# A two-layer adaLN block on one core: the order of VectorE's small root steps in the first attention

## The chip, the core and the metric

The kernel runs on one core of a Trainium2 chip. The metric is the device time of one execution in microseconds. Before the change, three runs gave 1322.71, 1323.15 and 1325.7 us; the median is 1323.15.

Engines are called as in the profile: PE is TensorE, DVE is VectorE, ACT is ScalarE, POOL is GpSimd, SP is the queue that issues the DMAs.

## The reference, cut to what matters

Two layers, each an attention and a feed-forward part, over x of shape 32 x 256 x 128. Only the first attention matters here. For each of the 32 sequences:

```python
h = _layernorm(x, axis=-1) * (1 + ca) + sa
# inside _L0_attn_ref, whose x is h
x_norm = _layernorm(x, gamma, beta)
q = (x_norm @ w_q).reshape(B, T, HEADS, HEAD_DIM).transpose(0, 2, 1, 3)
k = (x_norm @ w_k).reshape(B, T, HEADS, HEAD_DIM).transpose(0, 2, 1, 3)
v = (x @ w_v).reshape(B, T, HEADS, HEAD_DIM).transpose(0, 2, 1, 3)
q = _l2_normalize(q)
k = _l2_normalize(k)
align = jnp.einsum('bhqd,bhkd->bhqk', q, k)
resonance = 0.5 + 0.5 * jnp.tanh((align - COLLAPSE_THRESHOLD) * SHARPNESS)
```

There are thus two norms in front (of x, then of the modulated h) and a division of every query and key by its length. The gates of q and k, the product with v, the output projection and the gated residual follow.

## The kernel before, in words

The first attention works on one sequence b of 256 rows (two tiles of 128) per turn. It is a software pipeline written out by hand: in turn b, ACT computes the tanh of the scores of sequence b, PE the scores and heads of b, while the sequences b + 1, b + 2 and b + 3 are prepared and b - 1 and b - 2 are finished. Each engine has its own `step(b, p)`, called by `stepped` (line 76 ff.) for b = -3 to 33: the turns up to 3 and from 28 are unrolled, the 24 turns from 4 to 27 run as a hardware loop of two turns per round. Every engine's instructions run in the order in which its `step` issues them, and semaphores hold them until what they need is there. The change touches DVE's `step` alone.

What DVE does in a turn, in its order (names as in the profile; the lines are those of the helpers):

- `stats_1`, `norm_1a` (L429, L440): statistics and moments of x for b + 3. POOL then computes 1/sqrt(variance + eps) in `rstd` (L403 add, L407 power), which gives `a_rstd`.
- `residual`, `heads_out`, `values`, `logits_out` (L854, L848, L829, L810): outputs of PE for b - 2, b - 1, b + 1 and b + 2. `logits_out` is a copy of 128x64.
- `norm_1b` (L446): the normalised tiles `a_xhat` of x for b + 3, two instructions. They wait for `a_rstd`. POOL waits for them and runs a row of four larger instructions: `a_scaled` (L414), `a_h` (L419), `a_wo_gated` (L706) and the sum into X (L708).
- `square_sums` (L748): sums over 8 of the squares of q and k of b + 2, 64 per row. The squares come from ACT (L656).
- nine `newton_step`s: the reciprocal root of these 64 sums. Step 1 clamps (L754, `a_norm2c`), step 2 makes an integer seed (L758, `a_seed`), steps 3 to 9 are small products on 128x64 tiles (L761, L763, L765, L768, L771, L773, L777). Each waits for the semaphore of the one before.
- `keys_out`, `queries_out` (L836, L841): copies of the turned keys and queries `a_kT` and `a_qT` of b + 1 from PSUM.
- `stats_2`, `norm_2a` (L429, L438, L440): statistics and moments of h for b + 3. POOL answers again with L403 and L407.
- `norm_2b` (L446): the tiles `a_xn`. PE waits for them and for `a_h` in `turn` (L523), which stands ahead of the scores of the next turn in its queue.
- `scale`, `gate_sums`, `turned_out`, `split_high`, `split_low`, `double_keys`: the normalised q and k, and their two f16 parts.

The steps with `norm` and `stats` exist while b + 3 is a sequence, so up to b = 28. POOL's `gate_out` (L706, L708) runs from b = 0. POOL's order in a turn is `norm_1`, `modulate`, `gate_out`, `norm_2`, `double_queries`. SP loads `a_mod_norm` for a later sequence once `a_h` is done.

Of the kernel before, what the change touches and what calls it, by code (L numbers as in the profile page):

```python
# [60 lines left out]
def wait(eng, sem, n):  # L61

    if isinstance(n, int) and n <= 0:
        return
    eng.wait_ge(sem, n)  # L65
# [228 lines left out]
def attention_0(nc, ctx, dram, sbuf, psum):  # L294
# [72 lines left out]
    def tile(b, t):  # L367
        return X[:, bass.ds(b * TT + t, 1), :] if not isinstance(b, int) else X[:, b * TT + t:b * TT + t + 1, :]
# [10 lines left out]
    def there(b):  # L379
        return not isinstance(b, int) or 0 <= b < B  # L380
# [62 lines left out]
    def standardise(dve, n, src, dst, mom, rstd, rstd_done, done):  # L443
        dve.wait_ge(rstd_done, n + 1)
        for t in range(TT):
            last = nc.vector.tensor_scalar(dst[:, t, :], src(t), mom[:, t, 0:1], rstd[:, t:t + 1], ALU.subtract, ALU.mult)  # L446
        last.then_inc(done, 1)

    def stats_1(dve, n):
        if isinstance(n, int) and n < FIRST:  # L450
            dve.wait_ge(dram["first_x_loaded"][n], 16)
        else:
            dve.wait_ge(x_loaded, (n - FIRST) * 16 + 16)
        wait(dve, moments1_done, n)
        for t in range(TT):
            statistics(n, lambda t: tile(n, t)[:, 0, :], stats1, stats1_done, t)

    def norm_1a(dve, n):
        moments_of(dve, n, stats1, moments1, stats1_done, moments1_done, xhat_done)

    def norm_1b(dve, n):

        wait(dve, scaled_done, n)
        standardise(dve, n, lambda t: tile(n, t)[:, 0, :], xhat, moments1, rstd1, rstd1_done, xhat_done)

    def stats_2(dve, n, t):
        if t == 0:
            dve.wait_ge(h_done, n + 1)
            wait(dve, moments2_done, n)
        statistics(n, lambda t: h[:, t, :], stats2, stats2_done, t)  # L470

    def norm_2a(dve, n):
        moments_of(dve, n, stats2, moments2, stats2_done, moments2_done, xn_done)

    def norm_2b(dve, n):

        wait(dve, turned, n)
        standardise(dve, n, lambda t: h[:, t, :], xn, moments2, rstd2, rstd2_done, xn_done)
# [9 lines left out]
    def run():  # L488
        with nc.Block() as block:
# [247 lines left out]
            def _(dve):  # L737
                def turned_out(n, p):
                    dve.wait_ge(turned, n + 1)

                    wait(dve, vl_psum, n)
                    nc.vector.tensor_copy(hT[p][:, :], PT[:, 0:T]).then_inc(hT_done, 1)
                    nc.vector.tensor_scalar(xnT[:, :], PT[:, T:2 * T], gammacol[:, :], betacol[:, :], ALU.mult, ALU.add).then_inc(xnT_done, 1)

                def square_sums(n):
                    dve.wait_ge(squares_done, n + 1)
                    wait(dve, newton, n * RSQRT_STEPS)
                    nc.vector.tensor_reduce(norm2[:, :], squares[:, :, :], AX.X, ALU.add).then_inc(norm2_done, 1)  # L748
# [32 lines left out]
                def scale(n):  # L781
                    dve.wait_ge(newton, n * RSQRT_STEPS + RSQRT_STEPS)
                    wait(dve, lo_done, n)
                    nc.vector.tensor_tensor(qkn[:, :, :, :].rearrange("p k t (h d) -> p t k h d", d=HD),
                                            PQ.rearrange("p (t k h d) -> p t k h d", t=TT, k=2, d=HD),
                                            rnorm[:, :].rearrange("p (t k h) -> p t k h", t=TT, k=2).unsqueeze(4).broadcast_to([P, TT, 2, H, HD]),
                                            ALU.mult).then_inc(qkn_done, 1)
# [19 lines left out]
                def logits_out(n):  # L807
                    dve.wait_ge(vl_psum, n + 1)
                    wait(dve, gate_in_done, n)
                    nc.vector.tensor_copy(logits[:, :], PL).then_inc(logits_done, 1)  # L810
# [13 lines left out]
                def values(n, p):  # L824
                    dve.wait_ge(vl_psum, n + 2)
                    dve.wait_ge(gates_done, n + 1)

                    wait(dve, heads_done, n * G - G)
                    nc.vector.tensor_tensor(vdiag[p], PV.rearrange("p (a r d) -> p a r d", r=G, d=HD),  # L829
                                            gate_k[:, :].rearrange("p (a r) -> p a r", r=G).unsqueeze(3).broadcast_to([P, TT * G, G, HD]),  # L830
                                            ALU.mult).then_inc(values_done, 1)

                def keys_out(n, p):
                    dve.wait_ge(kstack_psum, n + 1)
                    wait(dve, scores_ready, n * CHUNKS - CHUNKS)
                    nc.vector.tensor_copy(kT[p][:, :, :].rearrange("p g k -> p (g k)"), PT16).then_inc(kT_done, 1)  # L836

                def queries_out(n, p):
                    dve.wait_ge(qstack_psum, n + 1)
                    wait(dve, scores_ready, n * CHUNKS - CHUNKS)  # L840
                    nc.vector.tensor_copy(qT[p][:, :, :].rearrange("p g k -> p (g k)"), PT16).then_inc(qT_done, 1)  # L841

                def heads_out(n):

                    dve.wait_ge(heads_done, n * G + G)
                    dve.wait_ge(gT_done, n + 1)
                    wait(dve, projected, n)
                    nc.vector.scalar_tensor_tensor(out=oT[:, :], in0=PO[:, 0:T], scalar=PO[:, T:UNIT], in1=gT[:, :],  # L848
                                                   op0=ALU.add, op1=ALU.mult).then_inc(oT_done, 1)

                def residual(n):
                    dve.wait_ge(projected, n + 1)
                    dve.wait_ge(x_biased, n + 1)
                    nc.vector.tensor_tensor(tiles(n), tiles(n), PP.rearrange("p (t d) -> p t d", t=TT), ALU.add).then_inc(x_done, 1)  # L854

                def step(b, p):
                    older, old, new, next_, turns = there(b - 2), there(b - 1), there(b + 1), there(b + 2), there(b + 3)
                    ahead = turns and not (isinstance(b, int) and b == -3)

                    def newton_of(*ks):  # L860
                        if next_:
                            for k in ks:
                                newton_step(b + 2, k)

                    if ahead:
                        stats_1(dve, b + 3)
                    if older:
                        residual(b - 2)
                    if ahead:
                        norm_1a(dve, b + 3)  # L870
                    if old:
                        heads_out(b - 1)
                    if new:
                        values(b + 1, 1 - p)
                    if next_:
                        logits_out(b + 2)
                    if ahead:
                        norm_1b(dve, b + 3)
                    if next_:
                        square_sums(b + 2)  # L880
                    newton_of(1)
                    if new:
                        keys_out(b + 1, 1 - p)
                    newton_of(2)
                    if ahead:
                        stats_2(dve, b + 3, 0)
                    newton_of(3)
                    if ahead:
                        stats_2(dve, b + 3, 1)
                    newton_of(4)  # L890
                    if ahead:
                        norm_2a(dve, b + 3)
                    newton_of(5, 6)
                    if new:
                        queries_out(b + 1, 1 - p)
                    newton_of(7, 8, 9)
                    if ahead:
                        norm_2b(dve, b + 3)
                    if next_:
                        scale(b + 2)  # L900
                        gate_sums(b + 2)
                    if turns:
                        turned_out(b + 3, 1 - p)
                    if next_:
                        split_high(b + 2, p)
                        split_low(b + 2, p)
                        double_keys(b + 2, p)
                    if isinstance(b, int) and b == B - 1:
                        bound_squares(dve)
# [2313 lines left out]
```

## Time and profile before

| what | value |
|---|---|
| median of three runs | 1323.15 us |
| the profiled execution | 1322.84 us, span 1321.0 us |
| PE busy | 1219.2 us (92%) |
| DVE busy | 1055.2 us (80%) |
| ACT busy | 933.7 us (71%) |
| POOL busy | 574.6 us (43%) |
| turns of the first attention (first to last tanh of scores) | 42.5 to 398.2 us |

The span is that of the engines' instructions; the time of an execution lies a little above it. The shares of busy time are means over all stages. The first attention takes a good quarter of the span, and in the middle of it, from 200 to 300 us, PE is busy for 94.92 us, DVE for 93.04, ACT for 89.37 and POOL for 49.32, at a granted clock of 1.00 of TensorE. Four queues are close to full there, so the timelines and the waits tell more than the shares. In a timeline a row is one instruction or a few equal ones in a row (xN): start, duration, engine, line, operation, output and inputs. A DVE instruction that waits for nothing is recorded as starting up to 0.1 us before the end of the one in front of it.

### The profile page before, as it was taken

How to read it: one execution, taken by the hardware profiler on the slowest of the kernel's cores; microseconds unless marked ns; L12 is line 12 of the kernel's file. 1: busy time of each engine (PE TensorE's matmuls, PEld its weight loads, DVE VectorE, ACT ScalarE, POOL GpSimd, SP SyncE). 2: the span in 40 equal slices, each digit the busy share in tenths (PEclk: the TensorE clock that was granted, in tenths of full speed). 3: DMA queues.
4: the chain of work that ended last, by engine and by line, in shares of the span. 5: the costliest groups of instructions: out<-in, count | busy, mean ns of one | idle time of the engine just before them, and what ended most of it. 6: DMA issues, size and time to landing. Idle time of an engine off the chain costs nothing. (4 is left out here: it accounts for less than half of the span.)

```text
span 1321.0 us, 39879 instructions
## 1 busy us (share of the span) xinstructions
PE 1219.2 (92%) x13717; PEld 810.3 (61%) x13717; DVE 1055.2 (80%) x2935; ACT 933.7 (71%) x1338; POOL 574.6 (43%) x793
## 2 busy tenths in 40 slices
PE   3899999999996899997899999999879999999998
PEld 1555555555543677776555555555458878778776
DVE  5899999999965787766899999999746777777763
ACT  0698888888892556552588878788747676766765
POOL 2455444445421243322343343343236565655653
PEclk7799999999997999999899999999979999999999
DMA  4311111111002222200200000000000000000000
GB/s 126 141 35 32 33 35 36 36 36 36 28 10 49 58 50 59 59 17 4 105 14 16 12 12 16 12 12 17 6 2 9 9 16 8 16 8 16 16 8 25
DMA packets 47965, 40.68 MB, mean 31 GB/s; under 512 B 5376, under 2 KB 46688, under 8 KB 47360
## 3 DMA queue, kind: packets, MB, share of 16 engines
q1 hardware_dynamic: 47872, 39.45, 10.7%
q8 instruction: 57, 0.93, 0.3%
q14 instruction: 36, 0.29, 0.1%
HBM read 35.09 MB, written 4.34 MB: 30 GB/s over the span
## 5 line engine op out<-in xcount | busy, mean ns | idle before, releaser
L2416 ACT ACTIVATE a_probs<-psum_all 128x1024 f32<-128x1024 f32 x256 | 248.4, 1024 | 69.5 <-PE psum_all L2315 69.4
L683 ACT ACTIVATE probs<-psum_all,biases 128x1024 f32<-128x1024 f32 x256 | 272.5, 1115 | 32.8 <-PE psum_all L589 32.0
L2798 PE MATMUL psum_all<-ffn_hi,weights_r 128*128 128x512 f32 x704 | 283.8, 403 | 9.7 <-issue 4.5
L2798 PE MATMUL psum_all<-ffn_lo,weights_r 128*128 128x512 f32 x704 | 277.4, 394 | 0.0
L2758 POOL TENSOR_TENSOR ffn_lo<-ffn_full,ffn_hi 128x512 fp32r<-128x512 f32 x143 | 186.9, 1315 | 134.3 <-ACT ffn_hi L2875 97.8
L2798 PEld LDWEIGHTS psum_all<-ffn_hi,weights_r 128*128 128x128 f32 x704 | 133.7, 190 | 51.2 <-DVE ffn_full L2959 9.6
L2798 PEld LDWEIGHTS psum_all<-ffn_lo,weights_r 128*128 128x128 f32 x704 | 133.9, 190 | 25.8
L602 PE MATMUL psum_all<-probs,vpad 128*32 128x257 f32 x2048 | 138.0, 387 | 0.3 <-ACT probs L683 0.3
L2329 PE MATMUL psum_all<-a_probs,vpad 128*32 128x256 f32 x2048 | 137.7, 387 | 0.2 <-DVE a_sums L2494 0.2
L2887 ACT ACTIVATE ffn_full<-psum_all,scales 128x512 f32<-128x512 f32 x128 | 88.5, 691 | 68.0 <-PE psum_all L2798 67.9
L2758 DVE TENSOR_TENSOR ffn_lo<-ffn_full,ffn_hi 128x512 fp32r<-128x512 f32 x64 | 55.1, 861 | 80.3 <-ACT ffn_hi L2890 80.3
L713 POOL TENSOR_TENSOR a_stack<-a_stack,a_ones 128x512 f16<-128x512 f16 x32 | 36.6, 1145 | 123.0 <-DVE a_stack L800 123.0
L2890 ACT ACTIVATE ffn_hi<-psum_all,scales 128x512 fp32r<-128x512 f32 x128 | 87.4, 683 | 0.0
L589 PE MATMUL psum_all<-a_qT,a_kT 32*128 32x256 f16 x1024 | 76.1, 274 | 12.1 <-ACT probs L683 8.4
L2105 POOL TENSOR_TENSOR a_vareps<-a_moments,eps 128x2 f32<-128x2 f32 x32 | 6.2, 195 | 180.1 <-DVE a_moments L2132 180.1
L602 PEld LDWEIGHTS psum_all<-probs,vpad 128*32 128x32 f32 x2048 | 53.5, 109 | 49.9 <-issue 21.3
L2329 PEld LDWEIGHTS psum_all<-a_probs,vpad 128*32 128x32 f32 x2048 | 53.6, 109 | 49.8 <-issue 27.3
L2875 ACT CAST ffn_hi<-ffn_full 128x512 fp32r<-128x512 f32 x64 | 39.7, 621 | 38.2 <-DVE ffn_full L2959 38.0
L2315 PE MATMUL psum_all<-a_qT,a_kT 32*128 32x256 f16 x1024 | 64.7, 274 | 1.7 <-DVE a_qT L2489 0.9
L589 PEld LDWEIGHTS psum_all<-a_qT,a_kT 32*128 32x128 f16 x1024 | 22.9, 92 | 48.8 <-ACT probs L683 36.1
L2881 ACT ACTIVATE ffn_tanh<-psum_all,scales 128x512 f32<-128x512 f32 x64 | 43.6, 690 | 9.5 <-PE psum_all L2798 8.9
L2959 DVE SCALAR_TENSOR_TENSOR ffn_full<-psum_all,scales,ffn_gated 128x512 f32<-128x512 f32 x64 | 48.1, 751 | 2.3
(232 smaller groups left out, 2653.0 us busy)
## 6 DMA issues: line engine op xcount, KB each, us to landing
a_mod_gate<-modulation_table SPq DMA_DIRECT2D x64, 128.0 KB, 2.9
X<-in_x SPq DMA_DIRECT2D x32, 128.0 KB, 2.7
a_mod_norm<-modulation_table SPq DMA_DIRECT2D x32, 128.0 KB, 3.0
f<-in_f SPq DMA_DIRECT2D x2, 2048.0 KB, 10.3
e_mod_norm<-modulation_table SPq DMA_DIRECT2D x32, 128.0 KB, 3.1
out<-X SPq DMA_DIRECT2D x16, 256.0 KB, 2.3
e_gates<-modulation_table SPq DMA_DIRECT2D x32, 64.0 KB, 2.8
weights<-in_h SPq DMA_DIRECT2D x2, 1024.0 KB, 7.7
```

Of the source, the lines that this page charges most:

```text
L589: last = nc.tensor.matmul(SC[c % 2][:, (TT * r + kb) * T:(TT * r + kb + 1) * T], kT[p][rows, g, kb * P:(kb + 1) * P], qT[p][rows, g, :], s ...
L602: last = nc.tensor.matmul(PO[32 * r:32 * r + 32, :], vpad[p][:, kb, G * r + g, :], probs[:, (2 * g + r // 2) % 4, r % 2, kb, 0:UNIT], star ...
L683: nc.scalar.activation(probs[:, c % 4, :, :, 0:T].rearrange("p r k q -> p (r k) q"), SC[c % 2].rearrange("p (a q) -> p a q", q=T), ACT.Tan ...
L2315: last = nc.tensor.matmul(SC[c % 2][:, (TT * r + kb) * T:(TT * r + kb + 1) * T], kT[p][rows, g, kb * P:(kb + 1) * P], qT[p][rows, g, :], s ...
L2329: last = nc.tensor.matmul(PO[32 * r:32 * r + 32, s * T:(s + 1) * T], vpad[p][:, kb, G * r + g, :], probs[:, (2 * g + r // 2) % 4, r % 2, k ...
L2416: nc.scalar.activation(probs[:, c % 4, :, :, :].rearrange("p r k q -> p (r k q)"), SC[c % 2], ACT.Exp, scale=float(np.float32(1.0) / np.sq ...
L2758: subtract(lo[layer][:, k, :], full[layer][:, k, :], hi[layer][:, k, :].bitcast(F32), ALU.subtract).then_inc(done[layer], 1)
L2798: ins = nc.tensor.matmul(dst, weights[:, w0:w0 + P], part[layer][:, k, :], start=first and i == 0, stop=last and i == len(parts) - 1)
L2881: nc.scalar.activation(tanh[:, m % 2, :], pair(m)[0], ACT.Tanh, scale=scales[:, 0, m:m + 1]).then_inc(tanh_done, 1)
L2887: nc.scalar.activation(full[layer + 1][:, m, :], bank[m % 2], ACT.Gelu, scale=scales[:, 1 + layer, m:m + 1]).then_inc(full_done[layer + 1], 1)
L2890: nc.scalar.activation(hi[layer + 1][:, m, :], bank[m % 2], ACT.Gelu, scale=scales[:, 1 + layer, m:m + 1]).then_inc(hi_done[layer + 1], 1)
L2959: nc.vector.scalar_tensor_tensor(out=full[1][:, m, :], in0=pair(m)[1], scalar=scales[:, 1, m:m + 1], in1=gated[:, m % 2, :], op0=ALU.mult, ...
```

## The change

In DVE's `step`, two groups of instructions change places with what stands ahead of them.

```diff
                     if next_:
                         logits_out(b + 2)
-                    if ahead:
-                        norm_1b(dve, b + 3)
                     if next_:
                         square_sums(b + 2)
                     newton_of(1)
+                    if ahead:
+                        norm_1b(dve, b + 3)
                     if new:
                         keys_out(b + 1, 1 - p)
-                    newton_of(2)
+                    newton_of(2, 3, 4, 5, 6)
                     if ahead:
                         stats_2(dve, b + 3, 0)
-                    newton_of(3)
-                    if ahead:
                         stats_2(dve, b + 3, 1)
-                    newton_of(4)
-                    if ahead:
                         norm_2a(dve, b + 3)
-                    newton_of(5, 6)
                     if new:
                         queries_out(b + 1, 1 - p)
                     newton_of(7, 8, 9)
```

No instruction is added or removed, and the other engines' queues keep their order.

DVE's queue from the logits copy to the copy of the keys, in an unrolled turn, before:

```order
L810 COPY a_logits<-psum_all 128x64
L446 TENSOR_SCALAR a_xhat<-X,a_moments,a_rstd 128x128 x2
L748 TENSOR_REDUCE a_norm<-a_squares 128x64
L754 TENSOR_SCALAR a_norm2c<-a_norm 128x64
L836 COPY a_kT<-psum_all 128x1024
```

and with the change:

```order
L810 COPY a_logits<-psum_all 128x64
L748 TENSOR_REDUCE a_norm<-a_squares 128x64
L754 TENSOR_SCALAR a_norm2c<-a_norm 128x64
L446 TENSOR_SCALAR a_xhat<-X,a_moments,a_rstd 128x128 x2
L836 COPY a_kT<-psum_all 128x1024
```

The sums of squares (`a_norm`) and step 1 (`a_norm2c`) now stand ahead of the two `a_xhat` instructions for which POOL waits.

DVE's queue from the seed to the copy of the queries, in the same turn, before:

```order
L758 TENSOR_SCALAR a_seed<-a_norm2c 128x64
L429 BN_STATS a_stats<-a_h 128x6
L761 TENSOR_TENSOR a_newton<-a_seed 128x64
L429 BN_STATS a_stats<-a_h 128x6
L763 TENSOR_TENSOR a_newton<-a_newton,a_norm2c 128x64
L438 MEMSET a_unread 128x1
L440 BN_AGGR a_moments<-a_stats 128x2 x2
L765 SCALAR_TENSOR_TENSOR a_newton<-a_newton 128x64
L768 SCALAR_TENSOR_TENSOR a_newton<-a_newton,a_seed 128x64
L841 COPY a_qT<-psum_all 128x1024
```

and with the change:

```order
L758 TENSOR_SCALAR a_seed<-a_norm2c 128x64
L761 TENSOR_TENSOR a_newton<-a_seed 128x64
L763 TENSOR_TENSOR a_newton<-a_newton,a_norm2c 128x64
L765 SCALAR_TENSOR_TENSOR a_newton<-a_newton 128x64
L768 SCALAR_TENSOR_TENSOR a_newton<-a_newton,a_seed 128x64
L429 BN_STATS a_stats<-a_h 128x6 x2
L438 MEMSET a_unread 128x1
L440 BN_AGGR a_moments<-a_stats 128x2 x2
L841 COPY a_qT<-psum_all 128x1024
```

The steps 2 to 6 now follow each other directly, each waiting for the one before, and the statistics and moments of h stand behind them.

## Rows read from the trace of the kernel before

**Rows 1.** Timeline of DVE, one turn of the loop, from `a_xn` to `a_xn`.

```profile
211.71 0.60 DVE L446 TENSOR_SCALAR a_xn<-a_h,a_moments,a_rstd 128x128 f32<-128x128 f32 x2
...
216.95 0.21 DVE L810 COPY a_logits<-psum_all 128x64 f32<-128x64 f32 x1
217.48 0.60 DVE L446 TENSOR_SCALAR a_xhat<-X,a_moments,a_rstd 128x128 f32 x2 [0.32 <-POOL a_rstd L407]
218.00 0.68 DVE L748 TENSOR_REDUCE a_norm<-a_squares 128x64 f32<-128x512 f32 x1
218.72 0.38 DVE L754 TENSOR_SCALAR a_norm2c<-a_norm 128x64 f32<-128x64 f32 x1
219.02 0.68 DVE L836 COPY a_kT<-psum_all 128x1024 f16<-128x1024 f16 x1
219.62 0.29 DVE L758 TENSOR_SCALAR a_seed<-a_norm2c 128x64 int32<-128x64 int32 x1
...
220.11 0.26 DVE L761 TENSOR_TENSOR a_newton<-a_seed 128x64 f32<-128x64 f32 x1
...
220.49 0.56 DVE L763 TENSOR_TENSOR a_newton<-a_newton,a_norm2c 128x64 f32<-128x64 f32 x1
...
221.07 0.14 DVE L440 BATCH_NORM_AGGREGATE a_moments<-a_stats 128x2 f32<-128x6 f32 x1
...
221.50 0.68 DVE L841 COPY a_qT<-psum_all 128x1024 f16<-128x1024 f16 x1
...
222.76 0.60 DVE L446 TENSOR_SCALAR a_xn<-a_h,a_moments,a_rstd 128x128 f32<-128x128 f32 x2
```

**Rows 2.** List of waits, 88 to 355 us: who for whom: us, times, longest.

```profile
DVE a_xhat L446 <- POOL a_rstd L407: 7.7, 24, 0.3
```

**Rows 3.** Timelines of PE and ACT, the same turn.

```profile
212.41 0.41 PE L523 MATMUL psum_all<-ident,a_h 128*128 128x128 f32 x2 [0.26 <-issue]
...
216.49 0.58 ACT L656 ACTIVATE a_squares<-psum_all 128x512 f32<-128x512 f32 x1
```

**Rows 4.** Timeline of POOL, the same turn.

```profile
216.68 0.70 POOL L407 TENSOR_TENSOR a_rstd<-a_vareps,minus_half 128x2 f32<-128x2 f32 x1
218.32 0.73 POOL L414 TENSOR_TENSOR a_scaled<-a_xhat,a_mod_norm 128x256 f32<-128x256 f32 x1 [0.94 <-DVE a_xhat L446]
219.13 0.73 POOL L419 TENSOR_TENSOR a_h<-a_scaled,a_mod_norm 128x256 f32<-128x256 f32 x1
219.81 0.47 POOL L706 TENSOR_TENSOR a_wo_gated<-wo,a_mod_gate 128x128 f32<-128x128 f32 x1
220.23 0.74 POOL L708 TENSOR_TENSOR X<-X,a_mod_gate 128x256 f32 x1
221.36 0.28 POOL L403 TENSOR_TENSOR a_vareps<-a_moments,eps 128x2 f32<-128x2 f32 x1 [0.40 <-DVE a_moments L440]
221.72 0.71 POOL L407 TENSOR_TENSOR a_rstd<-a_vareps,minus_half 128x2 f32<-128x2 f32 x1
```

**Rows 5.** Timeline of DVE, a late turn without norms, POOL idle.

```profile
376.55 0.23 DVE L761 TENSOR_TENSOR a_newton<-a_seed 128x64 f32<-128x64 f32 x1
376.81 0.23 DVE L763 TENSOR_TENSOR a_newton<-a_newton,a_norm2c 128x64 f32<-128x64 f32 x1
```

**Rows 6.** Timelines of POOL and DVE in the setup.

```profile
14.48 0.85 POOL L419 TENSOR_TENSOR a_h<-a_scaled,a_mod_norm 128x256 f32<-128x256 f32 x1
...
14.67 0.70 DVE L278 SCALAR_TENSOR_TENSOR modcol<-col_sign,col_size 128x32 f32<-128x32 f32 x1
15.36 0.49 DVE L429 BATCH_NORM_STATS2 a_stats<-a_h 128x6 f32<-128x128 f32 x2
...
15.99 0.15 DVE L440 BATCH_NORM_AGGREGATE a_moments<-a_stats 128x2 f32<-128x6 f32 x1
```

**Rows 7.** Timelines of DVE and POOL, an early turn.

```profile
27.28 0.20 DVE L758 TENSOR_SCALAR a_seed<-a_norm2c 128x64 int32<-128x64 int32 x1
...
27.28 0.78 POOL L419 TENSOR_TENSOR a_h<-a_scaled,a_mod_norm 128x256 f32<-128x256 f32 x1
```

## The prediction

> **What bounds the kernel now.** Only the first attention stage is touched, so the views are read there alone. The timeline of VectorE (DVE) comes first, over one turn of the steady loop, from one normalised pair `a_xn` to the next [rows 1]. The reader is to see a queue that is never idle for long: the turn takes 222.76 - 211.71 = 11.05 us, and the only idle time put down in it is the 0.32 us before `a_xhat`, where DVE waits for GpSimd (POOL) to deliver `a_rstd`. The list of waits says that this happens in all 24 turns read, 7.7 us in total [rows 2]. TensorE's turning of h and xn starts only when `a_xn` has ended (212.31 to 212.41), with 0.26 us of idle time in front of it, and the next scores stand behind it in TensorE's queue [rows 3]. So the loop runs at the pace of DVE with POOL answering it: a turn is as long as the way from `a_xn` to `a_xn`, and whatever lengthens that way lengthens the stage. The other engines follow from TensorE's turning, at the same distance as before.
>
> The second thing to see is where DVE's small instructions end. `a_norm2c` starts at 218.72 and takes 0.38; it ends at 219.10, 0.05 after POOL's `a_scaled` (219.05). `a_seed` ends at 219.91, 0.05 after POOL's `a_h` (219.86). The first Newton product (L761) ends at 220.37, 0.09 after `a_wo_gated` (220.28), and the second (L763), 0.56 long, at 221.05, 0.08 after the sum into X (220.97) [rows 1, 4]. With POOL idle such products take 0.23 [rows 5]. **A small DVE instruction that meets a 128x128 or larger POOL instruction stands until that one ends.** Sums of squares, copies out of PSUM and the statistics are not held: `a_kT` keeps its 0.68 beside `a_scaled` and `a_h`. A scalar_tensor_tensor is held too: in the setup one took 0.70 and ended at 15.37, 0.04 after POOL's `a_h` (15.33) [rows 6]. In the order before, only two of the held instructions lose much, because POOL's four large instructions are spread over a stretch that DVE fills with statistics and copies.
>
> The Trainium skill says the same of the mechanism (page "SBUF — State Buffer", section "Who interferes with whom"): a DVE instruction with two SBUF inputs, or one in a two-port mode, shares a port pair with GpSimd, and whoever issues second is blocked for the other's whole instruction. It is a rule against this change, since it makes no exception for scalar_tensor_tensor, of which this trace has one good row; by it rival 3 below and its 1329 have no chance and the sum stays at 1348 or above, by the row alone that rival keeps a small one.
>
> **The change part by part.** All times count from E, the end of the logits copy (216.95 + 0.21 = 217.16). Before, `a_xn` starts at E + 5.60, and from `a_xn` to E nothing changes.
>
> *Sums of squares and step 1 go ahead of `a_xhat`.* The squares are ready (216.49 + 0.58 = 217.07 on ScalarE [rows 3]), so the sums start where DVE overlaps its neighbours, 0.08 before E, and take 0.68, to E + 0.60. `a_norm2c` follows 0.04 later and now meets no large POOL instruction: 0.23 as its kin with POOL idle [rows 5], to E + 0.87. `a_xhat` starts 0.08 before that, takes 0.60 and ends at E + 1.39; it ended at 218.08, E + 0.92. The wait of 0.32 is gone, and 0.15 of the holding of `a_norm2c`, but the tiles that POOL needs come 0.47 later.
>
> *POOL's row of four.* It starts 0.24 after `a_xhat` ends (218.32) and is undisturbed as before: `a_scaled` to +0.97, `a_h` from +1.05 to +1.79, `a_wo_gated` from +1.74 to +2.21, the sum into X to +2.90, all after the end of `a_xhat` [rows 4].
>
> *Steps 2 to 6 in a row, ahead of the statistics.* `a_kT` overlaps `a_xhat` by 0.08 and the seed can issue 0.60 later [rows 1], at +0.52: in the middle of `a_scaled`. It is held and ends at +1.02. Step 3 depends on it and issues 0.03 later (the spacing of chained steps: 376.78 to 376.81 [rows 5]), at +1.05, exactly when `a_h` starts. Who gets through is open; the one such tie in the trace, a seed and an `a_h` that both start at 27.28, went to DVE: the seed took 0.20 and `a_h` 0.78 in place of 0.74 [rows 7]. I take DVE. Step 3 runs 0.23 to +1.28 and pushes the end of `a_h` to +1.85. Step 4 issues at +1.31, is held, ends 0.08 behind `a_h`, +1.93. Step 5 issues at +1.96 into `a_wo_gated` (now +1.80 to +2.27) and ends at +2.35. Step 6 issues at +2.38 into the sum into X (+2.22 to +2.96) and ends at +3.04. Each step thus costs one POOL instruction, where statistics that are never held stood in between.
>
> *The statistics behind them.* They overlap step 6 by 0.08 and start at +2.96 (h has long been there). From the first statistics to the end of the aggregates, undivided, is 15.36 to 16.14 = 0.78 [rows 6]: moments at +3.74. Then POOL: 0.14 to its add (221.22 to 221.36), 0.36 to the power, 0.71, and 0.10 back to DVE (217.38 to 217.48): 1.31 [rows 1, 4], so `a_xn` can start at +5.05. DVE itself, with `a_qT` and steps 7 to 9 (222.76 - 221.50 = 1.26 from `a_qT`, which starts 0.06 before the moments), would be there at +4.94; a new wait of some 0.1 for `a_rstd` takes the place of the old one.
>
> *Sum.* `a_xn` at E + 1.39 + 5.05 = E + 6.44, against 5.60: **+0.84 us a turn**. The full pattern (norms ahead and POOL's gate_out) exists for b = 0 to 28, 29 turns: 24.4. Turns -2 and -1 have no gate_out and DVE waits for TensorE there; between 0 and 1.7 for both, I take 0.8. The last turns have no norms, and their order is the same. DMA issues and every other engine's order do not change; the load of `a_mod_norm` waits for `a_h`, half a microsecond later than now and still almost a turn ahead of its use, so it costs nothing. If that cover were gone, it would add to a turn only what it came late. Nothing else in the kernel is touched and later stages shift as they are. 1322.84 (the profiled execution's own time, 0.3 below the median shown) + 25.2 = **1348.0**.
>
> **Rivals.**
> 1. *`a_h` wins the tie.* Then step 3 ends at +1.87, step 4 is held by `a_wo_gated` to +2.29, step 5 by the sum into X to +2.98, and step 6 runs free to +3.24; the statistics start at +3.16, 0.20 later. 29 x 0.20 = 5.8: **1354**. The times are equal to a hundredth, and only one tie speaks against it.
> 2. *Faster: the holding does not move with the steps.* If the long records were due to something in their old places and the chained steps took their free 0.26 each, step 6 would end at +1.74, the statistics would start at +1.83 on `a_h`, the moments be done at +2.61, and POOL's own row would decide: end of the sum into X +2.90, add 0.03 behind it, 0.36, 0.71, 0.10, `a_xn` at +4.10, E + 5.49 against 5.60. 29 x -0.11 = -3.2: **1320**, the removed wait being won. It decides the sign from the point at which steps 3 to 6 lose less than some 0.8 us in all to POOL. Against it: four different instructions in one turn end behind four different POOL instructions [rows 1, 4].
> 3. *scalar_tensor_tensor is let through when both inputs are small tiles.* Steps 5 and 6 free: step 6 ends +2.41, moments +3.11, `a_xn` +4.42, +0.21 a turn: **1329**. One row speaks against it [rows 6].
> 4. *No effect:* the later `a_xn` is swallowed elsewhere. TensorE idles only 0.26 before it, so it could swallow nothing that is late: **1323**.
>
> **How the numbers follow.** Forecast 0.50, rival 1 0.30, a mixture of both or a step more or less held 0.05, rival 3 0.06, rival 2 0.06, rival 4 0.03. About 0.2% (2.6 us) is what a measurement of this kernel tells from no change, so rival 2 counts as faster and rival 4 as same. The range takes in forecast and rival 1 with the open sizes: the first turns (0 to 1.7), 0.05 a turn for each spacing that I took from its neighbours; and downwards one step that slips through a gap, a POOL instruction of 0.47 less per turn in half the turns, 7 us: 1340 to 1357.
>
> **What would show it.** In the timeline after: a turn of about 11.9 in place of 11.05; `a_xhat` with no idle time before it and a start at E + 0.79; `a_norm2c` at 0.23; seed about 0.5, step 3 about 0.21 (0.8 for rival 1), step 4 about 0.6, step 5 about 0.4, step 6 about 0.65 (0.23 for rival 1); TensorE's idle time before the turning near 1.1. All steps at 0.23 would make me wrong, and so would a shorter turn.

## The result, and the profile after

| | before | after |
|---|---|---|
| median of four runs | 1323.05 us (1322.71 to 1325.7) | 1359.45 us (1356.21 to 1361.69) |
| ratio, with its 95% interval | | 1.0266 [1.0242, 1.0290] |
| the profiled execution | 1322.84 us, span 1321.0 us | 1359.0 us, span 1357.1 us |
| turns of the steady loop | 11.05 and 11.48 us | 12.16 and 12.46 us |

The change makes the kernel slower by 36.4 us. The direction was forecast; the size, 25 us, was not: the result lies 2.5 us above the upper end of the range. The turns come in two lengths that alternate, so a turn of one kind is compared below with the same kind, or a pair of turns with a pair (before 22.53, after 24.62).

The page of the profile after:

```profile
span 1357.1 us, 39879 instructions
PE 1220.6 (90%) x13717; PEld 810.0 (60%) x13717; DVE 1086.2 (80%) x2935; ACT 932.6 (69%) x1338; POOL 571.7 (42%) x793
```

DVE runs the same number of instructions on the same tiles, and yet its busy time is 31.0 us above the 1055.2 of before, while PE and ACT stay where they were and POOL falls by 2.9. Instructions that stand in a queue of their own engine count as idle time; instructions that have issued and are held count as busy. So most of the loss hides in DVE's busy column: over the pair of turns around 230 us the records of steps 3 to 6 add up to 4.16 us where they had 2.48 before, while step 1 fell from 0.75 to 0.40. A smaller part of the growth is overlap between neighbours that chained steps no longer have.

The timeline of DVE after, one loop turn from `a_xn` to `a_xn`, to be read against [rows 1]:

```profile
230.99 0.60 DVE L446 TENSOR_SCALAR a_xn<-a_h,a_moments,a_rstd 128x128 f32<-128x128 f32 x2
...
236.23 0.21 DVE L810 COPY a_logits<-psum_all 128x64 f32<-128x64 f32 x1
236.48 0.69 DVE L748 TENSOR_REDUCE a_norm<-a_squares 128x64 f32<-128x512 f32 x1
237.20 0.20 DVE L754 TENSOR_SCALAR a_norm2c<-a_norm 128x64 f32<-128x64 f32 x1
237.31 0.60 DVE L446 TENSOR_SCALAR a_xhat<-X,a_moments,a_rstd 128x128 f32 x2
238.01 0.69 DVE L836 COPY a_kT<-psum_all 128x1024 f16<-128x1024 f16 x1
238.61 0.30 DVE L758 TENSOR_SCALAR a_seed<-a_norm2c 128x64 int32<-128x64 int32 x1
238.95 0.82 DVE L761 TENSOR_TENSOR a_newton<-a_seed 128x64 f32<-128x64 f32 x1
239.81 0.38 DVE L763 TENSOR_TENSOR a_newton<-a_newton,a_norm2c 128x64 f32<-128x64 f32 x1
240.22 0.66 DVE L765 SCALAR_TENSOR_TENSOR a_newton<-a_newton 128x64 f32<-128x64 f32 x1
240.91 0.22 DVE L768 SCALAR_TENSOR_TENSOR a_newton<-a_newton,a_seed 128x64 f32<-128x64 f32 x1
241.05 0.48 DVE L429 BATCH_NORM_STATS2 a_stats<-a_h 128x6 f32<-128x128 f32 x2
...
243.15 0.60 DVE L446 TENSOR_SCALAR a_xn<-a_h,a_moments,a_rstd 128x128 f32<-128x128 f32 x2
```

and of POOL beside it, against [rows 4]:

```profile
238.14 0.73 POOL L414 TENSOR_TENSOR a_scaled<-a_xhat,a_mod_norm 128x256 f32<-128x256 f32 x1 [1.48 <-DVE a_xhat L446]
238.94 0.75 POOL L419 TENSOR_TENSOR a_h<-a_scaled,a_mod_norm 128x256 f32<-128x256 f32 x1
239.65 0.46 POOL L706 TENSOR_TENSOR a_wo_gated<-wo,a_mod_gate 128x128 f32<-128x128 f32 x1
240.06 0.73 POOL L708 TENSOR_TENSOR X<-X,a_mod_gate 128x256 f32 x1
242.06 0.19 POOL L403 TENSOR_TENSOR a_vareps<-a_moments,eps 128x2 f32<-128x2 f32 x1 [1.26 <-DVE a_moments L440]
242.33 0.71 POOL L407 TENSOR_TENSOR a_rstd<-a_vareps,minus_half 128x2 f32<-128x2 f32 x1
```

Put the two side by side by their ends. Step 3 (L761) ends at 239.77, 0.08 after `a_h` (239.69). Step 4 (L763) ends at 240.19, 0.08 after `a_wo_gated` (240.11). Step 5 (L765) ends at 240.88, 0.09 after the sum into X (240.79). Step 6 (L768) finds POOL idle and takes 0.22. Three small products in a chain now each stand behind one of POOL's large instructions. `a_norm2c`, which stood behind `a_scaled` before, runs free in 0.20, and the wait of 0.32 before `a_xhat` is gone. A POOL record does not hold by its length alone: beside `a_rstd`, 0.71 long but on 128x2, steps 7 to 9 keep 0.21 to 0.23 in both kernels. Before, E (the end of the logits copy) to `a_xn` was 5.60; here E is 236.44 and `a_xn` starts at 243.15, E + 6.71.

The list of waits after, 88 to 370 us:

```profile
ACT probs L683 <- PE psum_all L589: 45.4, 25, 2.3
...
POOL a_scaled L414 <- DVE a_xhat L446: 35.6, 23, 2.8
...
PE psum_all L523 <- DVE a_xn L446: 28.1, 22, 1.4
```

The row of [rows 2] is no longer in it. In its place TensorE waits for `a_xn`, 28.1 / 22 = 1.28 us each time, where it idled 0.26 before [rows 3], and the tanh of ACT waits longer behind TensorE.

**Where the 36.1 us of span went.** The first `a_xn` comes 0.3 later than before. The three intervals that follow it (turns -2, -1 and 0) are 14.18, 12.99 and 13.72 long against 13.02, 11.87 and 12.38: +3.6. The 28 turns after that run from 58.58 to 404.44, against 54.66 to 368.88: +31.6. Two of the 28 are over a microsecond longer than their kind (13.65 and 13.88, against 12.16 to 12.57), which makes some 2.6; what is left is 29.0, or 1.04 a turn. The last `a_xn` is thus 35.6 late, and another 0.5 comes behind it.

### The profile page after: what moved, and what is told of

The parts are those of the page before. It is cut to its first block and busy times, and to the rows that moved or that the text cites. A ratio compares the mean times of both kernels' runs of the same rounds, so it can differ in the third digit from the quotient of the medians.

```text
span 1357.1 us, 39879 instructions
## 1 busy us (share of the span) xinstructions
PE 1220.6 (90%) x13717; PEld 810.0 (60%) x13717; DVE 1086.2 (80%) x2935; ACT 932.6 (69%) x1338; POOL 571.7 (42%) x793
## 5 line engine op out<-in xcount | busy, mean ns | idle before, releaser
L602 PEld LDWEIGHTS psum_all<-probs,vpad 128*32 128x32 f32 x2048 | 53.8, 109 | 50.3 <-issue 22.4
L523 PE MATMUL psum_all<-ident,a_h 128*128 128x128 f32 x64 | 13.9, 300 | 53.4 <-DVE a_xn L446 39.6
L589 PEld LDWEIGHTS psum_all<-a_qT,a_kT 32*128 32x128 f16 x1024 | 22.5, 92 | 50.0 <-ACT probs L683 31.3
```

The costliest lines, as they stand in the source:

```text
L589: last = nc.tensor.matmul(SC[c % 2][:, (TT * r + kb) * T:(TT * r + kb + 1) * T], kT[p][rows, g, kb * P:(kb + 1) * P], qT[p][rows, g, :], s ...
L602: last = nc.tensor.matmul(PO[32 * r:32 * r + 32, :], vpad[p][:, kb, G * r + g, :], probs[:, (2 * g + r // 2) % 4, r % 2, kb, 0:UNIT], star ...
```

## The experiments

**x1 and x2: each half of the change alone.** x1 moves only the sums of squares and step 1:

```diff
                         logits_out(b + 2)
-                    if ahead:
-                        norm_1b(dve, b + 3)
                     if next_:
                         square_sums(b + 2)
                     newton_of(1)
+                    if ahead:
+                        norm_1b(dve, b + 3)
```

> Only the sums of squares and step 1 go ahead of a_xhat; steps 2 to 6 stay between the statistics. Theory (the way from a_xn to a_xn through POOL, with DVE steps held by POOL's large instructions): a_xhat ends 0.47 later, the rest keeps its distance of 4.68 to it, so +0.45 to 0.5 us a turn, 31 turns, +14 to 16 us: about 1338, with step 3 near 0.26 and step 4 near 0.56 as before. Rival (the chained steps alone cost the time, the later tiles are hidden): within 3 us of 1323.

Measured: 1340.56 us, ratio 1.0130 [1.0105, 1.0154]. A pair of turns is 23.54, +0.50 a turn. DVE's timeline shows `a_xhat` with no wait, and the later steps as they were before, free and held in the same places:

```profile
203.69 0.60 DVE L446 TENSOR_SCALAR a_xhat<-X,a_moments,a_rstd 128x128 f32 x2
...
206.30 0.26 DVE L761 TENSOR_TENSOR a_newton<-a_seed 128x64 f32<-128x64 f32 x1
...
206.69 0.56 DVE L763 TENSOR_TENSOR a_newton<-a_newton,a_norm2c 128x64 f32<-128x64 f32 x1
```

x2 leaves `norm_1b` where it was and makes only the second move:

```diff
-                    newton_of(2)
+                    newton_of(2, 3, 4, 5, 6)
                     if ahead:
                         stats_2(dve, b + 3, 0)
-                    newton_of(3)
-                    if ahead:
                         stats_2(dve, b + 3, 1)
-                    newton_of(4)
-                    if ahead:
                         norm_2a(dve, b + 3)
-                    newton_of(5, 6)
```

> Only steps 2 to 6 go ahead of the statistics of h; a_xhat keeps its place and its wait of 0.32. Theory of holding: the seed ends behind a_h, step 3 behind a_wo_gated, step 4 behind the sum into X, steps 5 and 6 free (0.2 each), the statistics come 0.5 to 0.6 later and a_xn 0.6 to 0.75 later a turn: +18 to 23 us, about 1343. Rival (chaining alone, 0.1 us for each of three dependences that were covered): +0.3 a turn, about 1332, with all steps at 0.2 to 0.26.

Measured: 1346.95 us, ratio 1.0174 [1.0151, 1.0198]. A pair is 24.20, +0.83 a turn. DVE's timeline:

```profile
210.25 0.29 DVE L758 TENSOR_SCALAR a_seed<-a_norm2c 128x64 int32<-128x64 int32 x1
210.57 0.42 DVE L761 TENSOR_TENSOR a_newton<-a_seed 128x64 f32<-128x64 f32 x1
211.02 0.65 DVE L763 TENSOR_TENSOR a_newton<-a_newton,a_norm2c 128x64 f32<-128x64 f32 x1
```

and POOL's beside it:

```profile
210.44 0.47 POOL L706 TENSOR_TENSOR a_wo_gated<-wo,a_mod_gate 128x128 f32<-128x128 f32 x1
210.86 0.73 POOL L708 TENSOR_TENSOR X<-X,a_mod_gate 128x256 f32 x1
```

In x2 the steps are held where that was expected; the price is a little above the expected 0.6 to 0.75. Both halves cost, and they do not add up: 0.50 + 0.83 = 1.33, and the whole change costs 1.04. In x2 the sums of squares still stand behind `a_xhat`, so the chain arrives later in POOL's row of four: step 3 has to wait only for `a_wo_gated` (0.42) and step 4 for the sum into X (0.65). Step 6 ends 3.48 after `a_xhat` (208.12 + 0.60); with both halves it ends 3.22 after it (241.13 - 237.91). The last step that is held ends with POOL's row in both, 2.95 and 2.97 after `a_xhat`, and that place is the same whether the chain arrives early or late.

**x3 and x4: POOL's `gate_out` out of the stretch.** On POOL `gate_out` goes behind `norm_2` and waits for `a_xn`, and on DVE `gate_sums` goes behind `turned_out`; x3 does this to the changed kernel, x4 to the kernel before. POOL's part of the edit:

```diff
-                    if there(b):
-                        gate_out(b, p)
                     if fresh:
                         norm_2(pool, b + 3)
+                        pool.wait_ge(xn_done, b + 4)
+                    if there(b):
+                        gate_out(b, p)
```

> The changed kernel with POOL's a_wo_gated and the sum into X moved behind a_xn (and DVE's gate sums behind the two copies of turned h and xn, so that they do not sit under them). Theory of holding: step 3 is still held by a_h (0.8), steps 4 to 6 fall to 0.2 to 0.25 each, a_xn comes about 0.65 us earlier a turn than in the changed kernel: -19 us, about 1340. Rival (chained steps are slow by themselves): steps 4 and 5 keep 0.38 and 0.65, time stays at 1359.

> The kernel before with the same move of POOL's a_wo_gated and the sum into X behind a_xn and of DVE's gate sums. Theory of holding: step 4 falls from 0.56 to 0.2, step 3 from 0.26 to 0.21, a_xn 0.3 to 0.4 us earlier a turn until TensorE, which idles only 0.26 before its turning, becomes the bound: 5 to 10 us less, about 1315. Rival (DVE's steps do not decide, or the moved instructions hold others as long): 1323 or slower.

Measured: x3 1341.06 us, 1.0132 [1.0109, 1.0156], a pair 23.71; x4 1320.37 us, 0.9980 [0.9963, 0.9998], a pair 22.36. In x3 (lines are one further down) only the step beside `a_h` is still held:

```profile
207.79 0.81 DVE L762 TENSOR_TENSOR a_newton<-a_seed 128x64 f32<-128x64 f32 x1
208.63 0.23 DVE L764 TENSOR_TENSOR a_newton<-a_newton,a_norm2c 128x64 f32<-128x64 f32 x1
208.89 0.22 DVE L766 SCALAR_TENSOR_TENSOR a_newton<-a_newton 128x64 f32<-128x64 f32 x1
```

Nothing was done to DVE's chain itself, and steps 4 and 5 fall from 0.38 and 0.66 to 0.23 and 0.22 as soon as POOL is idle beside them. That rules out a cost of the new places themselves. With `gate_out` away the change costs 1341.06 - 1320.37 = 20.7 us, where it cost 36.4; about 0.68 a turn, (23.71 - 22.36) / 2. x4 itself gained less than was expected of it; x7 below shows why.

**x5: `a_h` a little later, so that DVE should win the tie.** Two writes of 128x1 stand between `a_scaled` and `a_h` on POOL; the results stay the same.

```diff
+        for i in range(2):
+            nc.gpsimd.memset(pause[:, i:i + 1], 0.0)
         pool.wait_ge(scaled_done, n + 1)
```

> The changed kernel with two memsets of 128x1 on POOL between a_scaled and a_h, so that a_h starts some hundredths to 0.1 us later. Theory (whoever starts first keeps the other out, and in the changed kernel a_h starts just before step 3): step 3 now comes first and falls from 0.82 to 0.23, a_h takes about 0.83 as in the one turn where that happened, steps 4 to 6 are then held 0.65, 0.38 and 0.65, and a turn is some 0.1 us shorter or equal: 1354 to 1359. Rival (step 3 is slow for another reason): step 3 stays at 0.82, time 1359 to 1363.

Measured: 1361.33 us, 1.0281 [1.0251, 1.0310]. It missed its aim. In the timelines of POOL and of DVE:

```profile
215.12 0.14 POOL L418 MEMSET a_pause<- 128x1 f32 x2
215.27 0.74 POOL L422 TENSOR_TENSOR a_h<-a_scaled,a_mod_norm 128x256 f32<-128x256 f32 x1
```

```profile
214.93 0.38 DVE L761 TENSOR_SCALAR a_seed<-a_norm2c 128x64 int32<-128x64 int32 x1
215.35 0.75 DVE L764 TENSOR_TENSOR a_newton<-a_seed 128x64 f32<-128x64 f32 x1
```

The writes hold the seed as well: it takes 0.38 in place of 0.30 and ends 0.05 after them (215.31, 215.26). So step 3 moved as far as `a_h` did, and now issues 0.08 behind it instead of level with it. The tie was not tested, only turned into a clear loss, and turns of 12.16 and 12.46 as in the kernel after say that a clear loss costs what a lost tie costs.

**x6: TensorE kept at work while it waits for `a_xn`.** From b = 1 on, four small matmuls into a bank that is overwritten later fill part of the idle time before `turn`; the results stay the same.

```diff
+                                if not isinstance(b, int) or b >= 1:
+                                    wait(pe, qT_done, b + 2)
+                                    keep_busy(nc, PT, ident16, 4)
                                 turn(b + 3)
```

> The changed kernel with four 512-column matmuls of the identity on PE ahead of each turning of h and xn from b = 1 on, into the bank that the turning fills next. They leave the results alone. Theory: two of the 36 us come from single turns (192.7 and 267.9 us) in which PE's granted clock falls to half after its idle time; with PE filled the clock stays at full speed, the turns stay near 12.15 and 12.5, and the time is 2 to 4 us less, 1355 to 1358, with less spread between runs. Rival (the long turns have another cause, or the filling delays the turning): no gain, 1359 or more.

What it is about shows in the kernel after. Its two long turns begin with matmuls that are slow, in the timeline of PE:

```profile
194.52 1.83 PE L602 MATMUL psum_all<-probs,vpad 128*32 128x257 f32 x16
```

against, in the turn at 231 us of the same kernel:

```profile
232.59 1.08 PE L602 MATMUL psum_all<-probs,vpad 128*32 128x257 f32 x16
```

and in the windows (from:to, us, busy time of PE, PEld, DVE, ACT and POOL, granted clock, DMA share, GB/s):

```profile
193.00:198.50 5.50, 4.94 (x36) 3.01 (x37) 4.65 (x16) 3.14 (x6) 1.71 (x3) 0.69 0.03 7
198.50:220.00 21.50, 18.37 (x238) 10.33 (x237) 19.59 (x63) 17.11 (x21) 9.39 (x16) 1.00 0.13 37
```

TensorE's granted clock falls to half (1.2 in place of 2.4 GHz) for 3.4 us at about 194.7 and again at 269.8, each time some 1.2 us after the end of an idle time of 1.28 and 1.27 us before the turning. The other turns of the loop have such an idle time too, mostly 1.19 to 1.37 us, and no fall. Before the change, with at most 0.45 idle there, the clock never falls between 49 and 404 us. In x2, with 0.97 to 1.25 idle there, it does not fall in the loop either.

Measured: x6 1356.39 us, 1.0248 [1.0224, 1.0272], and no fall of the clock in the stage. That x6 is about 3 us below the kernel after is not the clock's alone: its turns show the tie going both ways. In 15 of the 30 turns in which step 3 meets `a_h` DVE wins, as here (timelines of DVE, then of POOL):

```profile
211.94 0.22 DVE L764 TENSOR_TENSOR a_newton<-a_seed 128x64 f32<-128x64 f32 x1
212.19 0.65 DVE L766 TENSOR_TENSOR a_newton<-a_newton,a_norm2c 128x64 f32<-128x64 f32 x1
212.88 0.38 DVE L768 SCALAR_TENSOR_TENSOR a_newton<-a_newton 128x64 f32<-128x64 f32 x1
213.29 0.65 DVE L771 SCALAR_TENSOR_TENSOR a_newton<-a_newton,a_seed 128x64 f32<-128x64 f32 x1
```

```profile
211.93 0.83 POOL L419 TENSOR_TENSOR a_h<-a_scaled,a_mod_norm 128x256 f32<-128x256 f32 x1
```

Here `a_h` takes 0.83 in place of 0.75, step 3 is free, and steps 4, 5 and 6 are held by the three POOL instructions, which is the forecast's own picture. Such turns take 11.99 and 12.28; the turns of the same execution in which DVE loses take 12.17 and 12.46. So the tie is worth 0.17 to 0.18 a turn, and x6 shows it within one kernel. The 14 wins more than in the kernel after (2.4 us) and the two long turns saved (2.6) make 5.0, and the stage shows them: the last `a_xn` starts at 398.93 against 404.44. The span is only 3.1 shorter because what lies behind the last `a_xn` took 955.1 us against 952.7. No edit here touches that part, and in the eleven profiles it takes 948.4 to 955.6 us, so differences of a few microseconds are better read from the stage than from the whole time.

**x7: a version that beats both.** POOL's part of x4 alone, on the kernel before.

> The kernel before with POOL's a_wo_gated and the sum into X behind a_xn, DVE's gate sums left in their place. Theory: as x4_before_gate_late, 1319 to 1321; the gate sums are held until a_wo_gated ends (0.3 to 0.5), but DVE waits there for the turned tiles anyway. Rival: their holding is added to each turn, 0.3 x 29 = 9 us, about 1329.

Measured: 1315.53 us (1312.51 to 1317.81), 0.9937 [0.9918, 0.9955], some 4 us better than was expected. A pair of turns is 21.98, 0.28 a turn less than before. The timeline of DVE:

```profile
205.92 0.21 DVE L762 TENSOR_TENSOR a_newton<-a_seed 128x64 f32<-128x64 f32 x1
...
206.25 0.21 DVE L764 TENSOR_TENSOR a_newton<-a_newton,a_norm2c 128x64 f32<-128x64 f32 x1
```

and of POOL:

```profile
209.16 0.46 POOL L706 TENSOR_TENSOR a_wo_gated<-wo,a_mod_gate 128x128 f32<-128x128 f32 x1 [1.31 <-PE psum_all L613]
209.57 0.77 POOL L708 TENSOR_TENSOR X<-X,a_mod_gate 128x256 f32 x1
```

Step 4 takes 0.21 where it took 0.56 [rows 1]. `gate_out` now runs while DVE multiplies straight out of PSUM and copies, and those instructions keep their length; of that stretch only `a_gate_in` is longer in most turns, up to 0.34 where it has 0.26 in every turn before. In its timeline TensorE turns h without a wait, behind its own product:

```profile
208.29 0.71 PE L613 MATMUL psum_all<-a_wo_gated,a_oT 128*128 128x128 f32 x4
209.00 0.41 PE L523 MATMUL psum_all<-ident,a_h 128*128 128x128 f32 x2
```

x4 differs by the late `gate_sums` alone and is 4.8 us behind, though their runs overlap (1315.34 at the lowest, against 1317.81 at the highest of x7). In x4 DVE waits 0.17 a turn for the turned tiles, with the gate sums no longer standing in that gap, and its turns are 0.19 longer than those of x7: the wait accounts for most of the difference.

**x8: x7 with the first norm's moments ahead of the residual on DVE.** The aim is the wait for `a_rstd`, which x7 still has (8.0 us in 24 turns).

```diff
                         stats_1(dve, b + 3)
-                    if older:
-                        residual(b - 2)
                     if ahead:
                         norm_1a(dve, b + 3)
+                    if older:
+                        residual(b - 2)
```

> The kernel before with POOL's a_wo_gated and the sum into X behind a_xn, and DVE's moments of x ahead of the residual, so that POOL has a_rstd 0.3 us earlier. Theory: the wait of 0.33 before a_xhat shrinks to 0.1 or less; a turn falls from 10.75 to 10.6 at best, since TensorE has no idle time left before its turning: 1311 to 1315. Rival (TensorE is the bound already): no change against x7_before_gate_late_only, 1315.5.

Measured: 1313.92 us, 0.9919 [0.9891, 0.9947]. The wait is gone from the list of waits, and the time cannot be told from that of x7. The turns are 10.74 and 11.04, against 10.75 and 11.23, and the last `a_xn` starts at 359.91 against 361.52. So the wait of 0.33, the one that the change also removes, is worth about 0.1 a turn here and not its length: in x7 TensorE already turns h without a wait.

**x9: x7's edit on the changed kernel.**

> The changed kernel with POOL's a_wo_gated and the sum into X behind a_xn and nothing else moved. Theory of holding: step 3 keeps 0.82, steps 4 to 6 take 0.2 to 0.25, a turn of 11.45 to 11.6 in place of 12.15, 1335 to 1341; a little less than x3_after_gate_late, where the gate sums stood behind the copies. Rival (the moved POOL instructions hold as much in their new place): 1345 or more.

Measured: 1337.97 us, 1.0113 [1.0068, 1.0158]. Turns of the loop are 11.39 to 11.99. Its four runs spread from 1333.07 to 1346.57. Compared with x7, the change costs 22.4 us when `gate_out` is out of the way, much as between x3 and x4 (20.7); by the start of the last `a_xn` it is 22.5 and 21.4. Step 3 is held by `a_h` and takes 0.81 where it loses the tie; where it wins (11 turns), step 4 is held in its place and takes 0.65. A turn of the first kind, then one of the second:

```profile
205.98 0.81 DVE L762 TENSOR_TENSOR a_newton<-a_seed 128x64 f32<-128x64 f32 x1
206.82 0.23 DVE L764 TENSOR_TENSOR a_newton<-a_newton,a_norm2c 128x64 f32<-128x64 f32 x1
...
241.21 0.23 DVE L762 TENSOR_TENSOR a_newton<-a_seed 128x64 f32<-128x64 f32 x1
241.47 0.65 DVE L764 TENSOR_TENSOR a_newton<-a_newton,a_norm2c 128x64 f32<-128x64 f32 x1
```

So of the 36.4 us some 14 to 16 need `gate_out` beside the chain; the rest is the later `a_xhat` and the step that `a_h` holds.

## Why the prediction was wrong, and where it was right

**Right: the path.** The forecast took the time from `a_xn` to `a_xn` as the length of a turn, with nothing to swallow a later `a_xn`. TensorE's wait for `a_xn` grew from 0.26 to 1.28, and 1.04 a turn came through whole, so rival 4 is out.

**Right: `a_xhat` later.** Forecast E + 1.39, measured E + 1.47 (237.91). The forecast let the sums of squares start 0.08 before E. They start 0.04 after it: the squares end on ACT at 236.35, 0.09 before E as in the turn before the change, and from there to DVE's start 0.13 pass, for which the forecast had nothing. x1 prices this half by itself at 0.50 a turn, where 0.47 was forecast.

**Right: each POOL instruction holds one step of the chain.** x3 takes POOL's last two away and the two steps are free, which rules out rival 2. Step 5, a scalar_tensor_tensor on small tiles, takes 0.66 beside the sum into X and 0.22 without it, which rules out rival 3. The Trainium skill (page "SBUF — State Buffer", section "Who interferes with whom") makes no exception for such an instruction; the trace agrees, with that 0.66. What the forecast said of sizes ("128x128 or larger") is no bound: in x5 a write of 128x1 holds too.

**Wrong: the tie.** The failed step is "Who gets through is open; [...] I take DVE." In the profile after, step 3 and `a_h` meet in 30 turns, in 26 of them with starts within 0.01 of each other, and POOL gets through in 29. The one exception is at 202.36, where both have the same start in the timelines of DVE and POOL:

```profile
202.36 0.23 DVE L761 TENSOR_TENSOR a_newton<-a_seed 128x64 f32<-128x64 f32 x1
```

```profile
202.36 0.83 POOL L419 TENSOR_TENSOR a_h<-a_scaled,a_mod_norm 128x256 f32<-128x256 f32 x1
```

That is rival 1, with its pattern of holding (0.82, 0.38, 0.66, 0.22) and its price: 0.84 + 0.20 = 1.04 a turn, measured 1.04. x6 measures the price within one kernel at 0.17 to 0.18. A single tie of other instructions [rows 7] was taken as evidence of who wins, and it was none. Since x6 lets DVE win in half of the turns with the chain itself unchanged, the outcome hangs on less than the profile's hundredth of a microsecond; what decides it stays open, and the one experiment that was to shift it (x5) did not test it.

**Mis-sized: the early turns.** "between 0 and 1.7 for both, I take 0.8" was for turns -2 and -1. They and the start of the first took 1.16 + 1.12 + 0.3 = 2.6, above even the upper bound, and turn 0 cost 1.34 and not 0.84; 0.20 of these 0.50 is the tie, the rest was not followed. The belief was that DVE waits for TensorE there anyway and so hides part of the delay. That wait lies ahead of the logits copy: it swallowed the 0.3 of the first `a_xn`, and nothing of what arises behind the copy. There `a_scaled` and `a_h` hold the chain without `gate_out` too: steps 3 and 4 take 0.75 and 0.77 in turn -2, step 3 takes 0.80 in turn -1, and from the end of the copy to `a_xn` the two turns lose 1.54 and 1.13.

**Missing: TensorE's clock.** Two falls, 2.6 us. They were named nowhere in the sum. The cover was visible before: 0.26 of idle time in front of the turning [rows 3], which the forecast itself let grow to 1.1, without asking what a longer idle time does to the clock. x6 fills the gap, and the falls are gone from its profile; one profile of each kernel shows this, together with x5's, where the gap is as long as after and the clock falls four times. That the idle time is what lets the clock fall is thus supported by x6, and what picks the turn stays open.

The bill, against the forecast's 25.2: + 5.6 for the lost tie (28 x 0.20) + 2.3 for the early turns + 2.6 for the clock + 0.5 behind the last `a_xn` = 36.2, against 36.1 of span. (The forecast puts the ends of `a_h`, `a_wo_gated` and the sum into X 0.01 later than [rows 4] has them, which changes nothing.) With the tie alone put right the forecast would have been rival 1's 1354, and inside the range; the early turns and the clock carried the result out of it.

## What to carry to other kernels

When small VectorE instructions on SBUF share a stretch with large GpSimd ones, read both timelines by their ends: a VectorE instruction that ends 0.05 to 0.09 after a GpSimd one was held, and its busy time is a wait. Put statistics, reductions and PSUM copies beside GpSimd's large instructions, and a chain of dependent small products where GpSimd is idle; or move the GpSimd work, which here (x7) gave 0.6% where bringing the chain forward lost 2.7%. What removing a visible wait of 0.32 a turn gains is not its length (x8 gained 0.1): ask what then stands in front of the work that others wait for.

## What the runs showed of the hardware that was not expected

- Who wins when both engines ask at once is not fixed. At starts that the profile puts within 0.01 us of each other it is 25 to 1 for POOL in the kernel after, 10 to 15 in x6 and 14 to 11 in x9. Where POOL started 0.02 or more ahead, it always won. One lost tie moves the turn by 0.17 to 0.20.
- Two writes of 128x1 on POOL, 0.14 together, hold a tensor_scalar of DVE until they end (x5: the seed 0.38 in place of 0.30). The power on 128x2, 0.71 long, holds nothing.
- An idle time of 1.2 to 1.4 us in every turn of some 12.2 is followed now and then, not always, by TensorE's clock at half for 3.4 us (twice in the kernel after, four times in x5), and such a turn is over a microsecond longer.
